# A decoder layer in fp32 on one core: first keys projected 256 tokens at a time, late layernorm chains shared between GpSimd and VectorE, turned tokens subtracted ahead of their sums

## The reference, cut to what matters

```python
x = x + attention(layernorm(x))          # 32 heads of 32, 8 key/value heads, rope, causal, biases
x = x + q8(layernorm(x)) @ q8(ctx)       # both operands rounded to 8 bits and clipped
h = layernorm(x)
x = x + h @ W_org.T + sum_e c[e] * (h @ down[e]) @ up[e]   # 8 adapters of rank 64
# c = softmax of keys @ (Wq @ mean of h over the tokens), one set for each batch element
```

## Time and profile before

| | us |
|---|---|
| median of 3 runs | 755.93 |
| lowest, highest | 753.75, 756.32 |
| the profiled execution | 755.29 |
| its span | 753.5 |
| TensorE busy | 682.1 (91%) |
| VectorE busy | 437.3 (58%) |
| ScalarE busy | 423.4 (56%) |
| GpSimd busy | 291.9 (39%) |
| mean granted TensorE clock | 0.961 |

### The profile page before, as it was taken

The page is one execution under the profiler, slowest core; times in us unless marked ns, Lnnn a source line. Parts: engine busy times, 40 slices in busy tenths (PEclk is TensorE's granted clock), DMA queues, the critical chain, the costliest instruction groups (busy, mean ns, idle before and its releaser), DMA issues.

```text
span 753.5 us, 12965 instructions
## 1 busy us (share of the span) xinstructions
PE 682.1 (91%) x4608; PEld 546.9 (73%) x4608; DVE 437.3 (58%) x1167; ACT 423.4 (56%) x1025; POOL 291.9 (39%) x340
## 2 busy tenths in 40 slices
PE   4999699999999899998888687998999696799998
PEld 4997577798777678786656575676787474688886
DVE  5685478776877536566868655243336779831112
ACT  4235387878787757698785755563314772412320
POOL 2066754534443444464304601418414022425520
PEclk9999799999999999999999799999999897999999
DMA  7605755562445724325452220406225361423102
GB/s 241 226 30 184 238 175 170 169 192 84 137 124 179 220 53 127 109 72 165 150 149 60 97 68 2 139 1 223 67 80 191 112 202 49 141 70 112 43 15 98
DMA packets 43824, 93.49 MB, mean 124 GB/s; under 512 B 5488, under 2 KB 5872, under 8 KB 42224
## 3 DMA queue, kind: packets, MB, share of 16 engines
q1 hardware_dynamic: 40176, 76.94, 30.8%
q0 software_dynamic: 3584, 15.73, 8.5%
HBM read 72.72 MB, written 19.92 MB: 123 GB/s over the span
## 4 chain that ended last, share of the span: by engine, by line
PE 64%; DVE 13%; ACT 8%; POOL 6%; issue 5%; DMA 4%; DVEq 0%; ACTq 0%
PE dense L1026 40%; PE probt L920 7%; PE score L908 5%; PE pv L935 5%; PE score L1026 3%; POOL w_lo L1575 3%; DVE stats L1307 2%; ACT prob_all L1110 2%; PE probt L892 1%; ACT stage L1066 1%; ACT w_hi L1070 1%; DMA stage<-in_w_o 1%; DVE prob_all L1356 1%; PE misc L944 1%; DVE ln_s L831 1%
## 5 line engine op out<-in xcount | busy, mean ns | idle before, releaser
L1026 PE MATMUL dense<-w_hi,act_t 128*128 128x512 f32 (+1 forms) x684 | 229.0, 397 | 18.5 <-POOL w_lo L1575 5.9
L1263 DVE CUSTOM_DVE_ANT_0 prob_all<-score,mask_sb 128x128 f32<-128x128 f32 (+3 forms) x256 | 123.2, 487 | 130.0 <-PE score L908 128.1
L1575 POOL TENSOR_TENSOR w_lo<-stage,w_hi 128x512 fp32r<-128x512 f32 x85 | 111.5, 1319 | 216.3 <-ACT w_hi L1070 216.2
L1110 ACT ACTIVATE prob_all<-prob_all,neg_max 128x128 f32<-128x128 f32 (+3 forms) x256 | 142.8, 558 | 44.6 <-DVE neg_max L1263 43.4
L1026 PEld LDWEIGHTS dense<-w_hi,act_t 128*128 128x128 f32 x684 | 130.6, 196 | 44.6 <-issue 8.0
L1026 PE MATMUL dense<-act_t,w_hi 128*128 128x512 f32 x408 | 140.3, 426 | 4.3 <-POOL w_lo L1575 2.6
L1026 PE MATMUL dense<-w_lo,act_t 128*128 128x512 f32 (+1 forms) x372 | 136.6, 388 | 1.6 <-ACT w_lo L1075 1.4
L920 PE MATMUL probt<-ident_sb,prob_all 128*128 128x128 f32 x640 | 113.8, 277 | 4.6 <-ACT prob_all L1119 4.0
L908 PE MATMUL score<-k_stack,q_stack 96*128 96x128 f32 (+3 forms) x256 | 90.7, 359 | 7.5 <-DMA q_stack<-rope_dram 4.9
L1119 ACT ACTIVATE prob_all<-probt 128x128 f32<-128x128 f32 (+3 forms) x160 | 68.7, 429 | 50.9 <-PE probt L920 50.3
L1070 ACT ACTIVATE w_hi<-stage 128x512 fp32r<-128x512 f32 x117 | 71.3, 622 | 44.1 <-PE dense L1026 30.7
(11 more groups left out here) (156 smaller groups left out, 895.6 us busy)
## 6 DMA issues: line engine op xcount, KB each, us to landing
q_stack<-rope_dram POOLq DMA_DIRECT2D x16, 768.0 KB, 7.6
stage<-in_w_qk SPq DMA_DIRECT2D x40, 256.0 KB, 2.9
rope_dram<-act_t SPq DMA_DIRECT2D x40, 256.0 KB, 3.2
stage<-in_w_o SPq DMA_DIRECT2D x32, 256.0 KB, 2.9
stage<-in_ctx_kv SPq DMA_DIRECT2D x24, 256.0 KB, 3.0
stage<-in_w_org SPq DMA_DIRECT2D x24, 256.0 KB, 2.8
xres<-in_x SPq DMA_DIRECT2D x8, 512.0 KB, 6.4
prob_all<-in_x SPq DMA_DIRECT2D x8, 512.0 KB, 6.1
```

The source lines that it names most:

```text
L1026: last = engine.matmul(dst, lhs, rhs, start=(k == 0 and c == 0), stop=(k == g.kts - 1 and c == len(pairs) - 1))
L1110: engine.activation(prob[:, u % P_SLOTS, 0:length], prob[:, u % P_SLOTS, 0:length], ACT.Exp, bias=neg_max[:, m:m + 1], scale=-1.0, accum_o ...
L1263: engine.tensor_tensor_reduce(prob[:, u % P_SLOTS, 0:length], score_bank[u % 2][:, 0:length], mask_sb[:, S - length:S], -1.0, HIGHEST, ALU ...
L1575: engine.tensor_tensor(slot_lo(p, 0, NW), raw_of(p), slot_hi(p, 0, NW).bitcast(F32), ALU.subtract).then_inc(g_piece, 1)
```

## The change

- The first keys of b = 0 are projected over two tiles of tokens at a time: 256 moving columns in place of 128. Slot 0 then holds v alone, slot 1 v and both key groups, slot 2 v alone, slot 3 v and both key groups. The turn of the next tile comes after the slot's last step in slots 0 and 2, and between the two key groups in slot 1.
- The turns of (1, 1) stand 6 slots later (12 to 40).
- `CHAINS_ON_VECTOR` goes by tile: of (3, 1), tiles 1 and 3 stay on VectorE, tiles 0 and 2 go to GpSimd.
- `tokens_low` subtracts first and sums after; what waits to turn into the bank again now waits for the sum's semaphore.
- Planner: in the units, turns keep 2 slots and 2.6 us apart, and none is put in the slot of an inverse's turn; elsewhere 1 slot and 2.6 us. `base` waits 2 slots and 1.6 us for its tokens (1 slot elsewhere). After the units a context sum waits 3.0 us after its last piece instead of 0.6.

The diff, with most of its context left out:

```diff
--- before
+++ after
@@ -43,6 +43,7 @@
 LATE_TURN_US = 5.0
+LATE_SUM_US = 3.0
 TOKENS_LAG = 1
@@ -51,7 +52,7 @@
 TERMS = 3
-CHAINS_ON_VECTOR = ((1, 0), (2, 1), (3, 1))
+CHAINS_ON_VECTOR = [(which, b, t) for which, b in ((1, 0), (2, 1)) for t in range(NT)] + [(3, 1, 1), (3, 1, 3)]
 EARLY_LAGS = 2.0, 3.5, 4.5, 6.0, 9.5
@@ -81,11 +82,13 @@
         v = self.add("v", 0, 0, self.TILES, KD, VW, 2)
-        ks = [self.add("k", 0, c, self.TILES, KD, P, 4) for c in range(2)]
+        ks = [self.add("k", 0, c, [0, 1], KD, P, 4) for c in range(2)]
+        self.token_ends = [0]
         for t in range(NT):
-            for g in [v] + ks:
-                self.add_tile(g, t)
-        self.token_steps = len(self.steps) // NT
+            self.add_tile(v, t)
+            for g in ks if t % 2 else []:
+                self.add_tile(g, t // 2)
+            self.token_ends.append(len(self.steps))
         for g in range(NKV):
@@ -206,11 +209,11 @@
         for t in range(NT):
-            self.note_steps(t, range(self.token_steps * t, self.token_steps * (t + 1)))
+            self.note_steps(t, range(*self.token_ends[t:t + 2]))
             self.at.append(now)
             self.due(t, now, False)
-            now += 7.0
-        s, credit = self.token_steps * NT, 0.0
+            now += 9.0 if t % 2 else 4.0
+        s, credit = self.token_ends[NT], 0.0
         self.first_norms()
@@ -323,12 +326,12 @@
             for half in range(2):
-                at = NT + 2 + 8 * t + 4 * half
+                at = NT + 8 + 8 * t + 4 * half
                 self.note("turn", at, (1, 1, t, half))
...
     def due_norms(self, j, now, unit):
-        if self.sums and self.past(j, ("centre", self.sums[0][2]), 1, now, 0.6):
+        if self.sums and self.past(j, ("centre", self.sums[0][2]), 1, now, 0.6 if unit else LATE_SUM_US):
             b, nb, p = self.sums[0]
@@ -398,9 +401,11 @@
+        if unit and (j - self.first_unit_slot - PV_LAG) % (NT * GROUP) == NT * GROUP - 1:
+            return False
         if other or not self.turned:
             return True
-        return self.past(j, self.turned[-1], 3 if unit else 1, now, 2.0)
+        return self.past(j, self.turned[-1], 2 if unit else 1, now, 2.6)
@@ -417,7 +422,7 @@
         if g.kind == "base":
-            return self.past(j, ("tokens", 3, g.b, n, k // 4), 1, now, 0.8)
+            return self.past(j, ("tokens", 3, g.b, n, k // 4), 2 if self.units_in(j) else 1, now, 1.6)
         if g.kind == "down":
@@ -668,9 +673,9 @@
-            order = [(1, 0), (1, 1), (2, 0), (3, 0), (2, 1), (3, 1)]
-            mine = (which, b) in CHAINS_ON_VECTOR
-            return NT * sum((o in CHAINS_ON_VECTOR) == mine for o in order[:order.index((which, b))]) + t
+            order = [(w, c, n) for w, c in ((1, 0), (1, 1), (2, 0), (3, 0), (2, 1), (3, 1)) for n in range(NT)]
+            mine = (which, b, t) in CHAINS_ON_VECTOR
+            return sum((o in CHAINS_ON_VECTOR) == mine for o in order[:order.index((which, b, t))])
@@ -879,7 +884,7 @@
                 elif which == 3:
-                    e.wait_ge(v_xt, low_no(3, 1, t - 1, half) + 1)
+                    e.wait_ge(v_sums, sums_no(1, t - 1, half) + 1)
                 elif which == 2:
@@ -891,8 +896,8 @@
                 last.then_inc(t_xt, 1)
-                if not own and which != 2:
-                    misc_free.append((v_xt, low_no(which, b, t, half) + 1))
+                if not own and which == 3:
+                    misc_free.append((v_sums, sums_no(b, t, half) + 1))
                 elif not own and half:
@@ -978,8 +983,10 @@
-                if g.kind == "v" or g.kind == "k" and g.b == 0:
+                if g.kind == "v":
                     e.wait_ge(v_xt, low_no(1, g.b, n, k // 4) + 1)
+                elif g.kind == "k" and g.b == 0:
+                    e.wait_ge(v_xt, low_no(1, 0, 2 * n + 1, k // 4) + 1)
                 elif g.kind in ("q", "k"):
@@ -998,7 +1005,7 @@
                 if g.kind in ("q", "k"):
-                    cols = m if g.b == 0 and g.kind == "k" else slice(0, S)
+                    cols = slice(2 * n * P, 2 * (n + 1) * P) if g.b == 0 and g.kind == "k" else slice(0, S)
                     hi, lo = act_t[NORM_T[g.b]][:, 0, k, cols], act_t[NORM_T[g.b]][:, 1, k, cols]
@@ -1015,7 +1022,7 @@
                 if g.kind == "k" and g.b == 0:
-                    dst = score_bank[g.nb][:, n * P:(n + 1) * P]
+                    dst = score_bank[g.nb][:, 2 * n * P:2 * (n + 1) * P]
                 else:
@@ -1041,12 +1048,15 @@
                 for s in range(first, end):
-                    if j < NT - 1 and s == first + plan.token_steps // 2:
+                    if j == 1 and s == first + 2 * KD:
                         for half in range(2):
...
                     step(s)
+                if j in (0, 2):
+                    for half in range(2):
+                        turn_tokens(1, 0, j + 1, half)
                 if 0 <= u - PV_LAG < UNITS and (u - PV_LAG) % GROUP == GROUP - 1:
@@ -1078,7 +1088,7 @@
                 src, dst = residual[b][:, t, :], xnorm[:, t % 2, :]
-                e.wait_ge(v_norm if (which, b) in CHAINS_ON_VECTOR else g_norm, norm_no(which, b, t) + 1)
+                e.wait_ge(v_norm if (which, b, t) in CHAINS_ON_VECTOR else g_norm, norm_no(which, b, t) + 1)
                 if which == 1:
@@ -1307,7 +1317,7 @@
                     wait_ln()
-                    if (which, b) not in CHAINS_ON_VECTOR:
+                    if (which, b, t) not in CHAINS_ON_VECTOR:
                         engine.bn_aggr(mean_var[:, t, :], stats[:, t, :, :]).then_inc(v_stats, 1)
@@ -1323,11 +1333,11 @@
                 e.wait_ge(a_xt, turned_no(which, b, t, half) + 1)
+                engine.tensor_tensor(lo, src, hi.bitcast(F32), ALU.subtract).then_inc(v_xt, 1)
                 if which == 3:
...
                     engine.tensor_reduce(tok_sum[:, t, 4 * half:4 * half + 4], src, AX_X, ALU.add).then_inc(v_sums, 1)
-                engine.tensor_tensor(lo, src, hi.bitcast(F32), ALU.subtract).then_inc(v_xt, 1)
@@ -1563,7 +1573,7 @@
             def norm_chain(which, b, t):
-                if (which, b) in CHAINS_ON_VECTOR:
+                if (which, b, t) in CHAINS_ON_VECTOR:
                     return
```

## The result

| | before | after |
|---|---|---|
| median | 754.84 us (4 runs, 753.02 to 756.32) | 732.24 us (4 runs, 731.89 to 736.95) |
| ratio | | 0.9716, 95% interval 0.9669 to 0.9763 |
| the profiled execution's span | 753.5 us | 730.5 us |

The account below looks back on a forecast made before the run. TensorE was taken to bound the kernel on the whole, VectorE from 617 to 650 us. Opening, units and the stretch behind them summed as 755.3 - 1.5 - 4 - 5.1 = 744.7 us; predicted 744.5 us, range 736 to 752 us.

Parts of the forecast that it names:

- Opening: Before the first score: wider keys cut TensorE's work by 9.6 us, GpSimd's chains start sooner; -1.5 us, ends -5 and +1.
- Units with (3, 0): Units with layernorm (3, 0): closer turns move dense work into empty slots and fill idle time at 410 to 475 us; -4 us.
- Subtraction first: Turned tokens: low parts come 0.6 us sooner in the units, within the -4 us; counted 0 behind the units.
- Behind the units: Stretch after the units: chains, subtraction order, context sums and last turns together give -5.1 us, ends -8 and -1.
- (a): Second batch's cross product: two chains moved off VectorE give 2 x 2.28 = 4.6 us.
- (d): Last turns behind the units: keeping 2.6 us between them moves one turn by a step, worth nothing.
- (c): Context sums behind the units: the first, placed later, costs +0.5 us; the second, leaving its place ahead of cross, gives -1.0 us.
- Rival 2: Units give nothing: waits for subtractions become waits of the next turn, which needs the sum; 748.7 us, chance 0.2.
- rival 5: Units: turns two slots apart lock the engines, costing 12.6 us at 1.8 us a turn; 761.3 us, chance 0.04.
- rival 6: Whole kernel: nothing of the gain arrives; 755 us, chance 0.04.
- Rival 4: More than counted: opening follows TensorE (-4 us) and the units fill 7 us; 739.2 us, chance 0.12.
- Rival 3: Port: GpSimd's chains stretch VectorE's corrections by 1.1 us at two more places; 746.9 us, chance 0.1.

Follow-up runs that it names:

- the filler: Zero-block-by-identity products added to the kernel before, at eight places where TensorE waits for turned tokens: eight each, 757.21 us (ratio 1.0024); three each, 755.82 us (0.9981).

## Why the prediction was wrong, step by step

**The reading of what bounds** held: what was won lies in the stretches in which TensorE had been idle, and from 666.9 us on nothing moved. The terms failed, the units' above all. The sentence "each idle stretch costs twice" stood in the prediction, from the earlier trace rows; the sum then priced the units' idle time once.

**Opening, forecast -1.5 us; measured +0.9 us at the first score, and nothing in the medians.** The mechanism was right: the chains of (1, 1) stood in the way. The size of their shift was wrong. They were to start 0.5 to 2.5 us sooner and started 0.6 us later:

```profile
42.10 0.22 POOL L829 TENSOR_SCALAR ln_s<-mean_var 128x1 f32<-128x1 f32 x1 [21.73 <-DVE mean_var L1321]
```

The step that failed is the one that counted v of tile 1 at either clock, 2.9 or 5.1 us, and then took the gain. TensorE paused twice ahead of it, 1.16 us for ScalarE and 1.92 us for VectorE's subtraction, and it then ran all at the low level; from the timeline, and from the chain of waits:

```profile
18.57 1.09 PE L897 MATMUL probt<-ident_sb,xres 128*128 128x128 f32 x8 [1.16 <-ACT xres L1106]
...
21.58 0.58 PE L1033 MATMUL dense<-w_hi,act_t 128*128 128x256 f32 x1 [1.92 <-DVE act_t L1336]
...
21.58 5.49 PE dense L1033 x24
```

So the turn of tile 2 came at 29.94 us, 2.0 us later than before (27.94), and the low parts of tile 3 at 38.95 us, 9.0 us behind it; by that distance the forecast's own late case, a turn at 29.5 us, gives 38.5 us and not its 38. From there VectorE's statistics, and with them the chains, came later and not sooner. GpSimd's chains then took 16.7 us for 16.1. The keys were done at 48.6 us and not at 45 to 47.5. The first score came after 88.3 us, which the text had named as a sign of error.

**Units with (3, 0), forecast -4 us (ends -8 and +8); measured -15.2 us.** This is the step that put the result outside the range. The planner's slots were worked out right: turns at 257, 260, 262, 265, 267, 269, 271 and 273, the last base steps 4 slots sooner. The term was priced over 65 us, from 410 to 475 us, as so much idle time filled. There the forecast held: TensorE idles 9.1 us in the 65 us from 412.2 us on after, under 10 as said. But the effect of the rules reached to the end of the down products at 548 us, and the price left out two things that the windows show: the work takes 7.1 us less (119.35 to 112.27 us, of the 15.2) at the higher clock, and idle time goes behind 475 us too (4.5 to 1.2 us). The low end of -8 us was "over half of the idle time" of that window, so the bound had the same flaw. The last unit's score comes 9.4 us sooner after cross (0) (85.4 us for 94.8), and 5.8 us more are won behind it (37.2 us for 43.0), where TensorE is busy all but 2.6 us, its clock goes from 0.96 to 1.00, and 12 of 233 matmuls have moved ahead. How much of the 15.2 us the clock gives by itself no run shows: the rules end idle time and raise the clock together, and the filler puts its own work in the place of what it frees.

**Subtraction first** was forecast as part of the -4 us. Alone it is worth 4.4 us, beside the rules nothing in this stretch.

**Behind the units, forecast -5.1 us (ends -8 and -1); measured -9.8 us** (202.26 to 192.50 us from the first take-out of out (1) to the last of all). Two terms were mis-sized. (a) The chains were forecast at 2 x 2.28 = 4.6 us and gave 7.5 us alone, 5.9 of them in cross (1). The 4.6 us are right for the chains; the sum left out that GpSimd, busy with them, makes its low parts behind VectorE's corrections and no longer beside one (1.1 us), and what follows in up (0, 1) (1.2 us) and in out (1) (0.5 us). (d) The last turns' distance was put at nothing, as one turn moved by a step. Two tiles' turns moved by a slot each, and the kernel with the spacing alone takes 2.1 us less from the last take-out of cross (1) to the first of base (1). The reading of the wait at 640.80 us as VectorE's was half of it: that take-out ended at 640.65 us, but GpSimd's low parts only at 640.79 us. The wait of 3.27 us was to fall to about 1 us. It stands at 0.41 us for tile 0, but one of its size remains, where tile 1's chain still runs on VectorE:

```profile
612.86 0.47 PE L1033 MATMUL dense<-k_stack,act_t 128*128 128x512 f32 x1 [0.41 <-DVE prob_all L1411]
...
618.15 0.79 PE L1033 MATMUL dense<-k_stack,act_t 128*128 128x512 f32 x1 [3.20 <-DVE prob_all L1411]
```

(c) The sums, +0.5 - 1.0 us, were right in size: too small to be told.

**The rivals.** Rival 2 (units give nothing), rival 5 (turns two slots apart lock the engines) and rival 6 fell. The wait that rivals 2 and 5 named does appear, in TensorE's waits from 410 to 475 us of the kernel after:

```profile
PE misc L897 <- DVE tok_sum L1340: 5.3, 4, 3.5
```

It is 1.3 us a time, over the 1 us that the text gave as a sign of error. Still the stretch is shorter: the wait replaced those of the dense steps, as in the earlier trace rows, and did not come on top. That sign was badly chosen. Rival 4 had the right direction in the units, at 7 us, and a gain of 4 us in the opening that did not come. Rival 3, the port, turned out the other way round. Beside GpSimd's chains VectorE's corrections take 0.75 us, as alone, and the chain's instructions, 0.34 us elsewhere, are what gets longer:

```profile
622.61 0.89 POOL L836 TENSOR_SCALAR ln_s<-ln_s 128x1 f32<-128x1 f32 x1
...
622.62 0.75 DVE L1366 SCALAR_TENSOR_TENSOR prob_all<-rope_sb,row_corr,prob_all 128x512 f32<-128x512 f32 x1
```

This one fell together with two of VectorE's low parts in the opening:

```profile
51.12 1.40 POOL L836 TENSOR_SCALAR ln_s<-ln_s 128x1 f32<-128x1 f32 x1
```

```profile
51.17 1.29 DVE L1253 TENSOR_TENSOR w_lo<-stage,w_hi 128x512 fp32r<-128x512 f32 x2
```

The Trainium skill, SBUF — State Buffer, "SBUF: two separate sides", has the exclusion of the two engines. The trace agrees: the tiny instruction ends 0.06 us behind the second low part. It shows who pays here, the chain, with 1.06 us each time, twice in the opening (51.12 and 55.84 us).

**The parts don't add.** Alone they give 1.1 (within its interval of nothing), 16.6, 4.4 and 9.2 us, 31 us in all, and together 21.4 us by the same count (23.7 us without the opening). The subtraction first and the rules overlap by nearly all of the former. The two rules are the reverse: 9.0 and 2.3 us alone, 16.6 together.

## What to carry to other kernels

When you end a wait of TensorE, ask first who sets the pace there. Where TensorE does, expect more than the idle time: the work behind it ran at the lower clock too, as v of tile 1 did in the opening. In the units' stretch 8.2 us less of idle time came with 7.1 us less of work, though no run parted the two. Where another engine sets the pace, count that engine's own time, as in cross (1), where a clock of 0.90 for 0.80 gave nothing and a chain or a shorter correction of VectorE gave its full length; and ask what else the engine that takes over the work will now do later. Follow a change of the planner's rules to the next stage that it delivers to, and not only through the window in which it is made. When an edit with less work gives nothing, look for the second bound close behind before dropping it: the keys over 256 tokens gave nothing, until the second batch's chains stood sooner in GpSimd's order, and then 6.5 us.

## What was not expected of the hardware

In the opening 24 matmuls of 256 columns took 5.49 us (their row is above), all at the 1.2 GHz level, against 2.92 us before. TensorE had come to the 2.4 GHz level at 16.96 us, ran at it for 0.5 us, and then paused for 1.16 and 1.92 us around eight transposes. The turn of tile 3, at 37.63 us, lies between pauses of 0.91 and 0.97 us, behind 9 us of work at the 2.4 GHz level; there the 24 matmuls of v that follow ran at that level still and took 3.0 us. The four pauses are 5.0 us and the lower clock 2.6 us: together 7.6 of the 9.6 us of work that the wide keys save, and the keys were done 1.7 us sooner.

A TensorE filler of 7.3 us over eight places raised the granted clock of a 138 us stretch from 0.93 to 0.94 and shortened the other work in it by 3.0 us; one of 16.9 us raised it to 0.96 and shortened that work by 6.2 us. Each unit of filler gave back some 0.4 of itself, so filler by itself did not pay.
